# Attention with relative positions: the order in which SyncE reads biases, writes probabilities and reads bands

## What is computed

```python
scores = einsum('bhqd,bhkd->bhqk', Q, K) / SCALE
scores = scores + einsum('bhqd,qkd->bhqk', Q, pek[idx]) / SCALE   # idx: clipped distance k - q
attn = softmax(where(causal, scores, -inf))
out = einsum('bhqk,bhkd->bhqd', attn, V) + einsum('bhqk,qkd->bhqd', attn, pev[idx])
x = layernorm(x + out @ Wo.T);  x = layernorm(x + ffn(x))
```

## Time and profile before

| | us |
|---|---|
| median of 3 runs | 5536.34 |
| the profiled execution | 5535.59 |
| its span (first to last instruction) | 5533.9 |
| `attention`, the part read here (500 to 4250 us) | 3750 |

### The profile page before, as it was taken

The page is one execution under the profiler, slowest core; times in us unless marked ns, Lnnn a source line. Parts: engine busy times, 40 slices in busy tenths (PEclk is TensorE's granted clock), DMA queues, the critical chain, the costliest instruction groups (busy, mean ns, idle before and its releaser), DMA issues. The chain is left out here.

```text
span 5533.9 us, 143122 instructions
## 1 busy us (share of the span) xinstructions
PE 5134.9 (93%) x49460; PEld 3347.5 (60%) x49460; DVE 3774.5 (68%) x8777; ACT 3425.3 (62%) x7512; POOL 1831.3 (33%) x2516
## 2 busy tenths in 40 slices
PE   9986999999999999999999999999999799999999
PEld 5554666666666666666666666666666455665665
DVE  5555777777777777777777777777777455555554
ACT  4445888878778887887877878778787211111111
POOL 3443333333333333333333333333333011111111
PEclk9997999999999999999999999999999899999999
DMA  7888999999999999999999999999999311111110
GB/s 223 254 252 264 329 323 324 332 316 323 321 324 324 325 323 321 324 328 325 322 325 327 322 321 327 316 323 327 324 322 304 99 61 56 50 61 61 61 55 32
DMA packets 654368, 1418.07 MB, mean 256 GB/s; under 512 B 64072, under 2 KB 362544, under 8 KB 641456
## 3 DMA queue, kind: packets, MB, share of 16 engines
q1 hardware_dynamic: 653744, 1409.89, 77.5%
HBM read 737.46 MB, written 672.14 MB: 255 GB/s over the span
## 5 line engine op out<-in xcount | busy, mean ns | idle before, releaser
L809 ACT ACTIVATE a_prob<-a_neg_s,a_neg_max 128x384 f32<-128x384 f32 (+1 forms) x1792 | 1081.1, 603 | 209.1 <-DVE a_neg_max L858 193.2
L524 DVE COPY a_p_t<-a_t_ps 128x512 f32<-128x512 f32 (+3 forms) x1536 | 952.5, 620 | 24.8 <-PE a_t_ps L773 23.9
L773 PE MATMUL a_t_ps<-a_ident,a_prob 128*128 128x128 f32 x5120 | 924.5, 280 | 31.5 <-DVE a_p_t L524 20.4
L858 DVE CUSTOM_DVE_ANT_1 a_neg_s<-a_s_ps,a_bias,a_far_neg 128x384 f32<-128x384 f32 x1280 | 791.0, 618 | 237.6 <-DVE a_far_neg L852 237.6
L706 PE MATMUL a_s_ps<-a_k,a_q 96*128 96x512 bf16 (+3 forms) x3072 | 852.7, 332 | 107.2 <-ACT a_far L813 105.1
L852 DVE TENSOR_REDUCE a_far_neg<-a_s_ps 128x1 f32<-128x640 f32 (+4 forms) x1280 | 708.8, 554 | 312.0 <-PE a_s_ps L706 178.5
L816 ACT ACTIVATE a_b_out<-a_t_ps 128x512 f32<-128x512 f32 (+1 forms) x1024 | 587.4, 574 | 384.4 <-PE a_t_ps L716 364.6
L734 PE MATMUL a_o_ps<-a_p_t,a_v 128*32 128x128 f32 x18432 | 782.0, 279 | 7.8 <-ACT a_o_t L821 0.2
L813 ACT ACTIVATE a_far<-a_s_ps,a_neg_max 128x640 f32<-128x640 f32 (+4 forms) x1280 | 730.6, 571 | 0.0
L816 ACT ACTIVATE a_p_t<-a_t_ps 128x512 f32<-128x512 f32 (+3 forms) x1536 | 672.8, 438 | 71.0 <-PE a_t_ps L773 53.4
L773 PE MATMUL a_t_ps<-a_ident,a_far 128*128 128x128 f32 x3840 | 662.5, 278 | 55.5 <-DVE a_p_t L524 52.2
(11 more groups left out here) (99 smaller groups left out, 6678.4 us busy)
## 6 DMA issues: line engine op xcount, KB each, us to landing
a_bias<-bias_scr SPq DMA_DIRECT2D x448, 576.0 KB, 7.8
prob_scr<-a_prob SPq DMA_DIRECT2D x448, 576.0 KB, 6.5
bias_scr<-a_b_out SPq DMA_DIRECT2D x448, 512.0 KB, 7.1
a_band<-prob_scr SPq DMA_DIRECT2D x448, 512.0 KB, 5.6
qk_scr<-p_parts SPq DMA_DIRECT2D x256, 192.0 KB, 3.4
v_scr<-p_v_out SPq DMA_DIRECT2D x256, 128.0 KB, 2.2
a_v<-v_scr SPq DMA_DIRECT2D x64, 512.0 KB, 8.9
attn_scr<-a_o_t SPq DMA_DIRECT2D x512, 64.0 KB, 7.4
```

What stands on the lines that cost most here:

```text
L524: copy(p_t[par][:, head, blocks[0] * P:(blocks[-1] + 1) * P], bank[:, 0:len(blocks) * P]) \
L773: mm = pe.transpose(bank[:, n * P:(n + 1) * P], prob_block(r, kk, head, b), ident[:, :])
L809: e = act.activation(near_prob(r, k, u, near(qb)), neg_s[:, u % 2, 0:w].rearrange("p (b c) -> p b c", c=P), ACT.Exp, bias=neg_max[:, u:u + ...
L858: dve.tensor_tensor_reduce(by_block(neg_s[:, u % 2, 0:w]), by_block(s_ps[:, u % 2, lo:lo + w]), near_bias(r, k, u, near(qb)), -1.0, begin, ...
```

## The change

In each step, the three large transfers at the beginning come in the opposite order: bias read of tile k+2, write of the probabilities of tile k-1, band read of tile k-2. Every transfer keeps its waits, its buffers and its size; saves, loads and the output stay behind them. No other engine's instructions change.

```diff
-                    if k >= 0 and ok(k - 2):
-
-                        par = k % 2
-                        if ok(k - 4):
-                            sp.wait_ge(r_mm, 2 * (T - 4) + 2)
-                        sp.wait_ge(set_ready, SET)
-                        sp.wait_ge(p_saved[(k - 2) % 4], quad(r, k - 2))
-                        n = run_of(q_block(k - 2))
-                        src = bass.AP(prob_scr.tensor, (k - 2) % 4 * P * WIDE + 1, [[n + P + 1, P], [1, n]])
-                        sp.dma_start(moved_band(k - 2), src).then_inc(p_loaded[par], 16)
-                    if k >= 0 and ok(k - 1):
-                        sp.wait_ge(wide_ready, T)
-                        n = run_of(q_block(k - 1)) + P
-                        rows = prob_scr[(k - 1) % 4, 0:P * n].rearrange("(q c) -> q c", c=n)
-                        sp.dma_start(rows, wide_prob(r, k - 1)).then_inc(p_saved[(k - 1) % 4], 16)
                     if k + 2 >= 0 and ok(k + 2):
...
                         sp.dma_start(bias[:, par, B_RAW:B_RAW + n], src).then_inc(b_loaded[par], 16)
+                    if k >= 0 and ok(k - 1):
+                        sp.wait_ge(wide_ready, T)
+                        n = run_of(q_block(k - 1)) + P
+                        rows = prob_scr[(k - 1) % 4, 0:P * n].rearrange("(q c) -> q c", c=n)
+                        sp.dma_start(rows, wide_prob(r, k - 1)).then_inc(p_saved[(k - 1) % 4], 16)
+                    if k >= 0 and ok(k - 2):
+
+                        par = k % 2
+                        if ok(k - 4):
+                            sp.wait_ge(r_mm, 2 * (T - 4) + 2)
+                        sp.wait_ge(set_ready, SET)
+                        sp.wait_ge(p_saved[(k - 2) % 4], quad(r, k - 2))
+                        n = run_of(q_block(k - 2))
+                        src = bass.AP(prob_scr.tensor, (k - 2) % 4 * P * WIDE + 1, [[n + P + 1, P], [1, n]])
+                        sp.dma_start(moved_band(k - 2), src).then_inc(p_loaded[par], 16)
                     if k % 2 and ok(k + LEAD):
```

## The result

The change makes the kernel slower: 5584.3 us (median of 4 runs, 5571.61 to 5593.18) against 5536.53 us for the kernel before, a ratio of 1.0084 with a 95% interval of 1.0061 to 1.0107. The forecast was 5481 us, range 5424 to 5565. The direction, the size and the range were wrong; what happened is rival B, between its mild form (5557) and its full price (5621).

What follows compares the result with a forecast made beforehand. TensorE (93.4%) and the DMA engines (0.97) were taken as nearly full. -75 us (bias waits) + 0 (write) + 20 (band waits) = -55 us, from 5535.59 to a forecast of 5481 us, range 5424 to 5565.

Steps and rivals of the forecast that it cites:

- rival B: TensorE at L780, large tiles: band read becomes late, up to 2.5 us a round, 5557 to 5621 us; chance 0.22.
- Part 1, bias first: VectorE's mask waits: bias read issued 2.4 to 4.2 us earlier, 75 of 107.5 us regained.
- The factor 0.7: VectorE before 2048.60: with the bias there it begins 1.14 us earlier, not 1.63; applied to all 107.5 us.
- The lower bound that I gave, 0: VectorE's bias waits: nothing regained, as TensorE sets the pace and time given back is waited for at scores.
- Rival A: `attention`: TensorE at 93.4% and DMA engines at 0.97 set the pace, no difference, 5536 us within 10; chance 0.18.
- Part 2, the write: SP's write of probabilities goes second, could go 1.1 us earlier behind one more transfer; costed at nothing by itself.
- Part 3, the band last: Band read behind 1152 KB in the DMA queue: some short TensorE waits, 20 us; bounds 0 and 160 us.
- all that is queued after it lands up to 2 us earlier: 3.5 - 2.0 = 1.5, less than the slack of 2.0: DMA queue: filling 2 us of idle time cuts the band's 3.5 us delay to 1.5, within TensorE's slack.
- It keeps its issue time within some tenths: SP's band read: L587 still ends its wait, and the two issues ahead mostly pass while SP would have waited.
- 0.3 us in each of 64 rounds: TensorE's band waits: some short waits, not one per round, summed to 20 us over the kernel.
- The ring: DMA queue, under rival B: each engine takes a ring's descriptors in order, so the band can't overtake the two transfers.
- The mark that I set for B: TensorE's row `PE a_t_ps L780 <- DMA a_band`: over 75 us would show that rival B has come true.

Runs made afterwards that it cites:

- write, band, bias: Against the kernel before, the three transfers go in the order write of the probabilities, band read, bias read: 5530.72 us, ratio 0.9994.
- The two pairs: Same waits within each, band behind two transfers or ahead of the bias read: all waits first, 5656.69 against 5547.64 us; write first, 5633.2 against 5530.72 us.
- the last mixed order: Against the kernel before, the change's order in odd steps and write, then band, then bias in even ones: 5515.37 us, ratio 0.9969.

## Why the prediction was wrong

**Part 1, bias first: the sign right, the size wrong.** VectorE's waits for the mask went, all of them in the stretch. The prediction valued them at 0.7 x 107.5 = 75 us. The runs bound them at 25 us, a factor of 0.23 or less. The factor 0.7 was read from one wait and looked only at what this wait needed (scores ready at 2047.46); the chain through the other engines is about as long, and VectorE's row for scores rose from 162.3 to 226.7 us. The lower bound that I gave, 0 ("TensorE sets the pace"), was nearer than the value taken. That one wait would have ended 1.14 us sooner says nothing of the steps behind it: what had to be asked was how much sooner the next 8 tiles would be done. Rival A was right in its reason, that both shares were near full, and wrong only in that the change could still lose.

**Part 2, the write: the nothing was wrong in one place, and a loop was missed.** I costed it at nothing, since nobody but L587 waits for its landing. But behind that wait stands the band read itself. For block 7 the write, now behind the bias read, landed later (8.1 us from issue for 7.3 in the round shown, 6.7 for 6.3 in the mean of all rounds), and the band went out later by nearly as much (0.7 us in that round). And that the write's place decides over the length of a loop from landing to landing did not stand in the prediction, and was the largest effect of all that I ran (+9.7%, with the lower clock in it).

**Part 3, the band last: the term that failed.** The working had the mechanism, the place (tiles 208 and 204, of blocks 7 and 5) and the bound of 160 us. The step that failed is "all that is queued after it lands up to 2 us earlier: 3.5 - 2.0 = 1.5, less than the slack of 2.0". In the changed kernel the band of this place landed 10.1 us from its issue where it had been 7.6, that is 2.5 us later and not 1.5. A second step failed with it: "It keeps its issue time within some tenths". Behind the end of `widen` the band went out 0.7 us later, since its own write took 0.8 us longer to land. And TensorE was ready for it 0.3 us sooner, which rival B had named: what the engines gain comes off the band's slack. 2.5 + 0.7 + 0.3 = 3.5 us against a slack of 2.0 leave 1.5; the trace has 1.47 us. The place was right and not a lucky pick: as means over all rounds (taken from the same rows, block by block) the band of block 7 goes out 7.1 us behind `widen` for 6.5 and lands after 10.1 us for 7.8, that of block 5 goes out at 7.5 for 6.8 and lands after 7.8 for 5.7. At block 5 the write is not what holds it, for it lands sooner than before; the band read is issued 3.2 us behind that landing (0.3 before), while SP issues the bias read, the write and the output and waits for ScalarE at a save.

The idle time of the DMA engines was filled (share 0.99, none of the stretches looked at below 0.82), yet it was not handed on in full to the band. One reason stands in SP's rows: it waited 744.6 us for `widen` and 350.6 us for the maxima, so the bias read and the write went out when the engines were ready, and could not fill idle time before that. And 20 us for the band waits, "0.3 us in each of 64 rounds", was a guess between 0 and 160; the trace shows 42.6 us in one stretch, and with 25 us of relief the 48 us of loss ask for some 73 us. The two rows of TensorE cover 60.3 us between them; some 12 us are left open.

**Part 3 and `widen`.** I priced the band behind the wait for `widen` at 1 us in one step of four. It became 744.6 us of SP's waits in all, yet write, band, bias shows it to be harmless where only one transfer is ahead of the band.

**The ring.** The Trainium skill, page "DMA: Bandwidth & Descriptors", section "Queues, rings and completion order", says that an engine takes a ring's descriptors in order. The two pairs agree with it, at 109 and 102 us, and it spoke for B more strongly than the chance of 0.22 allowed.

**What showed right.** Most of the signs named ahead came: mask waits at the first fill alone (24.3 us), bias waits of GpSimd under a half, more waits at `widen`, no stretch at 0.49 among those looked at. Two did not: the wait for the landing was to keep several hundred us and kept 34, and the DMA engines were to move more than 324 GB/s and moved 320. The mark that I set for B, over 75 us of band waits, was not reached by the row named; the loss came already at 42.6 us.

**Open.** Why the DMA engines' share rose while they moved less. That it isn't the cause is shown by the last mixed order (0.99 and 325 GB/s, and faster). That it was the fuller queue was only argued.

## What to carry to other kernels

In this kernel's one in-order queue, nearly full, the place of a transfer was its price. What I would carry over: give the first place to the transfer with the least slack at its reader, tile by tile, and not to the one that is waited for most. A wait of an engine that isn't the pace can be worth a fraction of its length (here 25 of 107.5 us at most), so make it vanish in a trial (halve its bytes) before anything is paid for it. And when an issuer waits for the landing of its own last write, whatever it puts ahead of the next write lengthens a loop: with the write second this cost nothing here, with the write behind the bias read 536 us.

## What the runs showed of the hardware that I had not expected

Queue order alone, with the same bytes and waits, moved this kernel by 102 and 109 us, and a bias read ahead of the write by 536 us (a lower granted clock included, 0.96 for 1.00). The DMA share went up to 0.99 in kernels that moved 320 GB/s (slower) and 325 GB/s (faster); it told nothing of which. The Trainium skill, page "Perfetto Trace Analysis", section "Identifying the Most-Contended Engine", warns of just this measure, and these runs agree.
